# First two images of a channel-attention kernel in an order of their own, and one store an image

## The reference

```python
v = _gn(x)                                 # group norm: 32 groups of 12 channels
w = xt @ qkv_w.T                           # 384 x 384, for each of 1024 pixels
norm = sqrt(sum(w*w over pixels))          # for each channel
s = sum((w / norm)**2 over a head's 32 channels)
Pi = softmax(s * temp, over the 12 heads)  # for each pixel
Pi_n = Pi / (sum(Pi over pixels) + 1e-8)
dots = sum(Pi_n * w*w over pixels)         # for each channel
out = -(w * Pi) / (1 + dots)
y = x + out @ out_w.T + out_b
```

## Time and profile before

| | |
|---|---|
| median of three runs | 877.63 us |
| the profiled execution | 877.32 us |
| its span, first to last instruction | 875.4 us |
| PE busy | 855.1 us (98%) |
| DVE busy | 746.8 us (85%) |
| ACT, POOL busy | 528.0 us (60%), 225.5 us (26%) |
| DMA | 158.47 MB, mean 181 GB/s |

### The profile page before, as it was taken

How to read it: one execution, slowest core, us unless ns; L and a number is a source line. 1 busy time by engine, 2 the same in 40 slices (tenths; PEclk the granted TensorE clock), 3 DMA queues, 4 the chain that set the end, 5 groups by cost and what they waited for, 6 DMA issues and landing times.

```text
span 875.4 us, 14196 instructions
## 1 busy us (share of the span) xinstructions
PE 855.1 (98%) x4298; PEld 682.2 (78%) x4298; DVE 746.8 (85%) x1377; ACT 528.0 (60%) x676; POOL 225.5 (26%) x101
## 2 busy tenths in 40 slices
PE   6799999999999999999999999999999999999996
PEld 6577787777787777787777787777787777787785
DVE  7598888898888898888889888898888889888767
ACT  3575556676555676555676555677555677555631
POOL 1321233321233331233331133331133331133300
PEclk9899999999999999999999999999999999999999
DMA  7316655446655445665445665545664545664424
GB/s 279 113 42 220 225 167 192 149 178 215 224 185 192 144 176 201 224 198 179 155 170 196 224 204 173 164 171 187 224 218 159 176 160 187 222 224 153 132 74 165
DMA packets 54996, 158.47 MB, mean 181 GB/s; under 512 B 21442, under 2 KB 25794, under 8 KB 51010
## 3 DMA queue, kind: packets, MB, share of 16 engines
q1 hardware_dynamic: 46192, 155.48, 51.9%
q10 hardware_dynamic: 8786, 2.77, 1.3%
HBM read 105.70 MB, written 52.53 MB: 181 GB/s over the span
## 4 chain that ended last, share of the span: by engine, by line
PE 93%; DVE 3%; DMA 2%; issue 1%; ACT 1%; SPq 0%; DVEq 0%; ACTq 0%
PE acc L498 87%; PE scores L579 5%; DMA PIB<-pi 1%; DMA bias<-in_L_conv_out_b 1%; DVE WS L769 1%; DVE stats L656 0%; PE acc L481 0%; DVE XL L714 0%; DVE UL L841 0%; DMA pi<-PIT 0%; DVE WV L812 0%; DVE W2L L630 0%; DVE W1L L630 0%; ACT WV L408 0%; DVE XN L706 0%
## 5 line engine op out<-in xcount | busy, mean ns | idle before, releaser
L349 POOL TENSOR_TENSOR XL<-XN,XH 128x1024 fp32r<-128x1024 f32 x93 | 222.5, 2409 | 589.8 <-ACT XH L427 589.8
L399 ACT ACTIVATE WS<-acc 128x1024 f32<-128x1024 f32 x96 | 97.9, 1020 | 227.4 <-PE acc L498 213.2
L498 PE MATMUL acc<-XH,W1H 128*128 128x512 f32 x576 | 179.1, 392 | 3.9 <-ACT XH L427 3.7
L498 PE MATMUL acc<-UH,W2H 128*128 128x512 f32 x576 | 178.1, 390 | 2.6 <-ACT UH L389 2.5
L498 PE MATMUL acc<-XH,W1L 128*128 128x512 f32 x576 | 178.4, 391 | 0.0
L498 PE MATMUL acc<-UH,W2L 128*128 128x512 f32 x576 | 177.8, 390 | 0.0
L849 DVE SCALAR_TENSOR_TENSOR X<-acc,bias,X 128x1024 f32<-128x1024 f32 x95 | 118.8, 1276 | 38.0 <-PE acc L498 38.0
L498 PE MATMUL acc<-UL,W2H 128*128 128x512 f32 x576 | 149.9, 396 | 0.0
L769 DVE CUSTOM_DVE_ANT_0 WS<-PIB,WS 128x1024 f32<-128x1024 f32 x96 | 117.3, 1223 | 36.5 <-DMA PIB<-pi 35.8
L498 PE MATMUL acc<-XL,W1H 128*128 128x512 f32 x576 | 147.2, 391 | 0.2 <-DVE XL L714 0.2
L389 ACT ACTIVATE UH<-WV 128x1024 fp32r<-128x1024 f32 x96 | 98.1, 1054 | 78.3 <-DVE WV L795 61.2
(11 more groups left out here) (84 smaller groups left out, 439.9 us busy)
## 6 DMA issues: line engine op xcount, KB each, us to landing
PIB<-pi SPq DMA_DIRECT2D x96, 528.0 KB, 6.1
out_y<-X SPq DMA_DIRECT2D x95, 512.0 KB, 7.4
X<-in_x SPq DMA_DIRECT2D x31, 1536.0 KB, 6.3
gathered<-stats_rows ACTq DMA_DIRECT2D x30, 72.0 KB, 6.7
pi<-PIT SPq DMA_DIRECT2D x96, 16.5 KB
X<-in_x SPq DMA_DIRECT2D x3, 512.0 KB, 4.6
WV<-in_L_conv_qkv_w SPq DMA_DIRECT2D x1, 576.0 KB, 6.7
WS<-in_L_conv_out_w SPq DMA_DIRECT2D x1, 576.0 KB, 7.6
```

The lines of the kernel that those rows point to most:

```text
L349: pool.tensor_tensor(XL[:, t, :], XN[:, t, :], XH[:, t, :].bitcast(F32), ALU.subtract).then_inc(xl_done, 1)
L399: act.activation(square_tile(i, t), acc[:, t, :], ACT.Square, accum_out=sumsq[:, t:t + 1]).then_inc(squared, 1)
L498: last = pe.matmul(out[:, h * BANK:(h + 1) * BANK], w[:, k, m * P:(m + 1) * P], r[:, k, h * BANK:(h + 1) * BANK], start=(n == 0 and k == 0 ...
```

## The change

Outside the steps of images 0 and 1, only the stores differ: an image is stored by one DMA of 1.5 MB when its third tile is finished, instead of three of 512 KB; the last image keeps its stores by parts. Images 0 and 1 leave the common `step`, and each engine has a list of its own for them:

- PE starts the first product of image 0 ahead of the transposes of the second weight matrix, which now follow the six XH terms of tile 0. Images 0 and 1 do their XH terms early and their XL terms late (`opening_product`). The head sums of image 0 stand after the second k of tile 0 of image 1, those of image 1 after six `idle_turns`, ahead of all of image 0's second product, which goes in the order of k (`product_by_k`).
- The group means of images 1 and 2 come from small matmuls too; the first image whose statistics go through DRAM is image 3 (`BY_MATMUL`).
- DVE makes XN and XH of image 1, which ACT made. ACT makes a second copy of the turned second weights in SBUF (`minus_w2`), from which POOL makes W2L; DVE made it from PSUM. POOL makes one of the three XL tiles of image 0.
- Image 0 is weighed by tiles like the last image (`attend_tile`).

```diff
+MM_AGGREGATED, MM_MEANS, MM_OFFSET, MM_SPREAD, MM_VARIANCES = range(1, 6)
+BY_MATMUL = 3
...
-IDLE_TURNS = (6, 3, 1, 15)
+IDLE_TURNS = (6, 4, 6, 15)
...
+        def by_tiles(j):
+
+            return not j.follows(1) or has(j) and not has(j + 1)
...
-                store(i - 2, 2)
+                if not i.follows(2):
+                    spread_pi(i)
+                    return
+                store(i - 2)
                 if has(i - 2) and has(i + 2):
-                    sp.wait_ge(y_stored, (i - 2).counts(T * 16, T * 16))
+                    sp.wait_ge(y_stored, (i - 2).counts(16, 16))
                     load(i + 2)
                 spread_pi(i)
-                store(i - 1, 0)
-                store(i - 1, 1)
-
-            write_stats(sp, FIRST + 1)
-            gather_stats(sp, FIRST + 1)
-            pipeline(sp, step, 0, B)
+
+            step(FIRST)
+            step(FIRST + 1)
+            write_stats(sp, FIRST + BY_MATMUL)
+            gather_stats(sp, FIRST + BY_MATMUL)
+            pipeline(sp, step, 2, B)
...
+            pool.wait_ge(xn_done, T)
+            pool.wait_ge(xh_done, T)
+            pool.wait_ge(xl_done, T - 1)
+            pool.tensor_tensor(XL[:, T - 1, :], XN[:, T - 1, :], XH[:, T - 1, :].bitcast(F32),
+                               ALU.subtract).then_inc(xl_done, 1)
+            for k in range(T):
+                pool.wait_ge(w2_copied, k + 1)
+                pool.tensor_tensor(W2L[:, k, :], minus_w2[:, k, :], W2H[:, k, :].bitcast(F32),
+                                   ALU.subtract).then_inc(w2_lo, 1)
+            pool.wait_ge(xn_done, 2 * T)
+            step(FIRST)
+            step(FIRST + 1)
+            pipeline(pool, step, 2, B)
...
+            def w2_higher():
+
+                for k in range(T):
+                    act.wait_ge(weights_turned, T + k + 1)
+                    act.activation(W2H[:, k, :], turned(T + k), ACT.Copy, scale=-1.0).then_inc(weights_hi, 1)
+                    act.activation(minus_w2[:, k, :], turned(T + k), ACT.Copy, scale=-1.0).then_inc(w2_copied, 1)
...
+                    act.wait_ge(m1_done, i.counts(T, t + 1))
+                    if not i.follows(2) and i.follows(1):
+                        act.wait_ge(w2_lo, T)
...
+            def first_steps():
+
+                zero, one, two = FIRST, FIRST + 1, FIRST + 2
+                square_w(zero, 0)
+                keep_w(zero, 0)
+                group_seeds(one)
+                square_w(zero, 1)
+                square_w(zero, 2)
+                keep_w(zero, 1)
+                keep_w(zero, 2)
+                exponentials(zero)
+                square_w(one, 0)
+                keep_w(one, 0)
+                group_seeds(two)
+                square_w(one, 1)
+                square_w(one, 2)
+                keep_w(one, 1)
+                u_hi(zero, 0)
+                keep_w(one, 2)
+                u_hi(zero, 1)
+                u_hi(zero, 2)
+                exponentials(one)
+                for t in range(T):
+                    normalise(two, t)
+                    x_hi(two, t)
+
+            w1_higher()
+            for t in range(T):
+                x_hi(FIRST, t)
+            w2_higher()
+            first_steps()
+            pipeline(act, step, 2, B)
...
+            def opening_product(i, order, between):
+
+                for t, ns in order:
+                    if ns == (0, 1) and i.follows(1):
+                        pe.wait_ge(squared, i.counts(T, t + 1 - T))
+                        pe.wait_ge(w_kept, i.counts(T, t + 1 - T))
+                    for k in range(T):
+                        for n in ns:
+                            if t == 0 and n == 0:
+                                pe.wait_ge(xh_done, i.counts(T, k + 1))
+                            if t == 0 and n == 2:
+                                pe.wait_ge(xl_done, i.counts(T, k + 1))
+                            last = term(acc[:, t, :], t, (W1H, W1L), (XH, XL), n, k)
+                        if t == T - 1 and ns == (0, 1):
+                            last.then_inc(xh_read, 1)
+                        elif ns == (2,) and k == T - 1:
+                            last.then_inc(m1_done, 1)
+                        for other in between.get((t, ns, k), ()):
+                            other()
+
...
+            group_variances(FIRST)
             turn_weights(range(1, T))
             idle_turns(acc[:, T - 1, 0:P], IDLE_TURNS[1])
-            pe.wait_ge(w2_mixed, 1)
-            pe.wait_ge(temp_kept, 1)
-            pe.wait_ge(gn_step, GN_AGGREGATED)
-            turn_weights(range(T, 2 * T))
-            idle_turns(acc[:, T - 1, 0:P], IDLE_TURNS[2])
+
+            def turn_w2():
+
+                pe.wait_ge(w2_mixed, 1)
+                pe.wait_ge(temp_kept, 1)
+                pe.wait_ge(gn_step, GN_AGGREGATED)
+                turn_weights(range(T, 2 * T))
+
+            hi, lo = (0, 1), (2,)
             pe.wait_ge(weights_lo, T)
-            pipeline(pe, step, 0, B)
+            opening_product(FIRST, [(0, hi), (1, hi), (0, lo), (2, hi), (1, lo), (2, lo)],
+                            {(0, hi, 2): [turn_w2],
+                             (0, lo, 2): [lambda: pe.wait_ge(w2_copied, T)],
+                             (2, hi, 0): [lambda: group_means(FIRST + 1)],
+                             (2, hi, 2): [lambda: group_variances(FIRST + 1)]})
+            opening_product(FIRST + 1, [(0, hi), (1, hi), (2, hi), (0, lo), (1, lo), (2, lo)],
+                            {(0, hi, 1): [lambda: head_sums(FIRST)],
+                             (0, lo, 2): [lambda: group_means(FIRST + 2)],
+                             (1, lo, 2): [lambda: group_variances(FIRST + 2)]})
+            pe.wait_ge(gn_step, (FIRST + 2).counts(GN_STEPS, GN_AGGREGATED))
+            idle_turns(small[:, P:2 * P], IDLE_TURNS[2])
+            head_sums(FIRST + 1)
+            pe.wait_ge(w2_lo, T)
+            product_by_k(FIRST)
+            pipeline(pe, step, 2, B)
...
+            for t in range(T):
+                normalise(FIRST, t)
+            for t in range(T - 1):
+                x_lo(FIRST, t)
+            one, two, three = FIRST + 1, FIRST + 2, FIRST + BY_MATMUL
+            group_stats(one, range(T))
+            part_moments(one)
             dve.wait_ge(temp_kept, 2)
             dve.tensor_tensor(head_temp[:], head_mask[:], temp_o[:].unsqueeze(2).to_broadcast([P, T, QUAD]),
                               ALU.mult).then_inc(temp_kept, 1)
-            pipeline(dve, step, 0, B)
+            part_spreads(one)
+            moments_kept(one)
+            group_norm(one)
+            for t in range(T):
+                x_hi(one, t)
+            normalise(one, 0)
+            normalise(one, 1)
+            head_sum_weights(FIRST)
+            normalise(one, 2)
+            softmax_shift(FIRST)
+            softmax_divide(FIRST)
+            group_stats(two, range(T))
+            part_moments(two)
+            part_spreads(two)
+            moments_kept(two)
+            group_norm(two)
+            attend_tile(FIRST, 0)
+            head_sum_weights(one)
+            attend_tile(FIRST, 1)
+            attend_tile(FIRST, 2)
+            dve.memset(wait_cell[:], 0.0).then_inc(u_step, U_STEPS - T)
+            softmax_shift(one)
+            u_lo(FIRST, 0)
+            softmax_divide(one)
+            u_lo(FIRST, 1)
+            u_lo(FIRST, 2)
+            finish(FIRST, 0)
+            finish(FIRST, 1)
+            group_stats(three, range(T))
+            pipeline(dve, step, 2, B)
```

More of the change, by code:

```diff
@@ L220, in has, with tile_steps, scale_of, wait_weighed @@
             return not isinstance(j.number, int) or 0 <= j.number < B
[L222 to L226, removed]
+        def by_tiles(j):
+            return not j.follows(1) or has(j) and not has(j + 1)
+        def tile_steps(j, t, steps):
+            return (T * TILE_STEPS if j.follows(1) else 0) + TILE_STEPS * t + steps
+        def scale_of(t):
+            return dots[:, 3, t:t + 1]
+        def wait_weighed(eng, j, t):
+            if by_tiles(j):
+                eng.wait_ge(tile_step, tile_steps(j, t, TILE_STEPS))
+            else:
+                eng.wait_ge(u_step, j.counts(U_STEPS, ATTENDED + t + 1))
+        def in_blocks(tile):
+            return tile.rearrange("p (b n) -> p b n", n=QUAD)
         def norm_of(j):
@@ new lines, in x_hi @@
+            def x_hi(j, t):
+                if has(j):
+                    rstd_j, shift_j = norm_of(j)
+                    act.wait_ge(gn_step, j.counts(GN_STEPS, GN_STEPS))
+                    if j.follows(1):
+                        act.wait_ge(m1_done, j.counts(T))
+                        act.wait_ge(xl_done, j.counts(T, t + 1 - T))
+                    act.activation(XH[:, t, :], x_tile(j, t), ACT.Identity, bias=shift_j,
+                                   scale=rstd_j).then_inc(xh_done, 1)
@@ L442, in step, with exponentials @@
+            def exponentials(i):
+                if has(i):
```

(22 more changed lines are left out.)

281 lines of the change are left out of this document (126 added, 155 removed).

## The result

The changed kernel takes **878.58 us** (median of 20 runs, 878.11 to 880.31). The kernel before, in the same session, took 877.36 (20 runs, 876.57 to 877.85). The ratio is 1.0017 by the statistic used here throughout, 95% interval 1.0010 to 1.0024 (the two medians alone give 1.0014): 1.2 us lost, no gain. By the measure that the prediction set (0.2% is what can be told from no change) this sits inside the band of no change; with 20 runs a side the interval shows that it is a small loss. The forecast was 876.2. The profiled run took 879.03, its span 877.2.

What follows compares the result with a forecast made beforehand. PE bounds the kernel (93% of the chain), with gains only in the opening: head sums of image 2 at 80.6 against 81.83, 1.25 us gained. 877.32 - 1.25 = 876.07, or 876.38 by the median; taken 876.2, own range 875.2 to 877.3.

Steps and rivals of the forecast that it cites:

- XH on DVE: Opening, image 1: 0.75 us a tile, priced like XN with float32 output (806 ns), not the two-operand 1220 ns.
- rival 3: Opening: XH on DVE takes 1.22 us, delaying the head sums of image 0 by 1.4, to 877.6; chance 0.08.
- Head sums of image 0: Opening: DVE ends their weights at 32.0, PE stands 1.7 us and begins them at 32.1.
- The distance between the head sums of images 2 and 31: Steady steps: 29 x 26.16 = 758.6 us; the prediction is wrong if it is not met within 0.5.
- rival 2: Steady steps win too, as stores no longer run beside pi: 28 x 0.03 = 0.8 us, 875.4; chance 0.15.
- rival 4: Steady steps: single store ends too late, load misses statistics; beyond some 4 us late, each microsecond costs 28; chance 0.03.
- cost the single store at nothing: Steady steps: the later store moves the same bytes; the next load has 7.4 us of cover, less the landing.
- The low parts come at 57.3, 59.9 and 61.05: Second product of image 0: DVE's three UL, with image 1's softmax (2.5 us) between; product ends at 64.3, against 66.67.
- the paragraph on stores, POOL, ACT and SP: Other engines and queues: single store costs nothing, POOL's W2L ends near 24.3, long before 50; program's end unchanged.
- The prediction's own signs of being wrong: Clock at 0.50 from 30 to 67 us, head sums of image 2 after 81.9, or image 2-to-31 distance off 758.6.
- Rival 1: Clock falls in PE's 2.9 us gap before image 1's head sums: 877.9, or 879.9 if slow 11 us; chance 0.25.
- Rival 5: Opening: nothing won, since DVE sets the head sums of image 2 and small waits reach 1.2 us: 877.4; chance 0.07.

Runs made afterwards that it cites:

- the first experiment: Changed kernel, with POOL starting XL of image 2 only after DVE's last UL of image 0: 876.55 us, ratio 0.9994 to the kernel before.
- the second experiment: Changed kernel, with POOL starting XL of image 2 after DVE's second UL of image 0, the third yet to run: 876.58 us, ratio 0.9994.

## Why the prediction was wrong

**What held.** The first matmul of the products came at 14.42 (forecast 14.65). XH on DVE took 0.75 us a tile, at the price of XN, not of UL, so rival 3 falls. Head sums of image 0 at 32.28 (32.1), of image 1 at 49.04 (48.8); all stations within 0.3 us over 50 us of opening. The distance between the head sums of images 2 and 31 was 758.45 (758.6 within 0.5), so rival 2 falls, and rival 4 with it: the single store does not come late. That this number came out right is in part luck. The prediction took it that both kernels give PE the same steps and cost the single store at nothing; with three stores the changed order takes 761.1 to 761.7 us for them. The new order made the steady steps dearer, the single store made that good, and neither was in the sum. PE's waits for XH and the slow clock from 36 to 44 us are gone too: that mechanism was right.

**The step that failed** is "The low parts come at 57.3, 59.9 and 61.05", and the paragraph on stores, POOL, ACT and SP behind it, which of POOL weighs only W2L ("ends near 24.3, long before 50") and so puts its XL of image 2 at nothing without a reason. The first two came at 57.4 and 59.9. The third ended at 63.2, since POOL's XL of image 2 starts as soon as ACT has made its XH, 58.9 us, and nothing in the sum asked what POOL does then. In the kernel before, the same three XL ran from 59.96 to 67.5 us, and DVE had softmax, statistics and `finish` there, none of which they lengthened. The change moved DVE's low parts beside them. The size fits: 2.2 us on one instruction, in a stretch in which, as the prediction itself said, DVE sets the head sums of image 2. The forecast for these plus 2.2 is 82.8 (measured 83.37), and the first experiment, which takes only this away, gives 81.00 and 876.55 us, where 80.6 and 876.2 had been forecast. The rest of the sum up to these head sums was right to 0.4 us. The prediction's own signs of being wrong came true with it: these head sums after 81.9, and 0.50 on the clock.

The Trainium skill states the mechanism, and the prediction missed it: "SBUF — State Buffer", section "SBUF: two separate sides", says that DVE and GpSimd share a port pair under a lock held for the whole instruction, and that a DVE instruction with two SBUF inputs contends for it with a GpSimd instruction that reads SBUF. These runs agree: 3.42 us instead of 1.21, and the turn of roles in the second experiment. With the lengths measured here, a rival would have read: POOL's XL beside UL, up to one XL of 2.4 us late, an estimate of 876.2 + 2.4 = 878.6. That it meets the measured time so closely is chance: the hold was 2.2 us, and other terms were off by 0.4.

**Rival 1 happened and was not the cause.** The clock fell to 0.50 behind the gap of 2.77 us (2.9 forecast) and was back between 53 and 54. It had been priced at 1.7 us for 7 slow us. It lasted some 4 and cost 0.2 us at most where POOL was out of the way, because DVE was what the next stations waited for: PE's lateness disappeared in its wait for the low parts. That the forecast time of this rival, 877.9, lies near the result is chance; holding the clock alone made the kernel slower still. Rival 5 named the engine: DVE did set the head sums of image 2, but through one hold of 2.2 us and not through small waits.

## What to carry to other kernels

When instructions of DVE move, list what **POOL** executes at their new time, not only who signals whom: a DVE instruction with two inputs in SBUF, or a TENSOR_SCALAR between SBUF tiles, may stand behind a whole POOL instruction. It shows as a longer duration with no idle time before it, so compare the longest of a group with its mean; one wait that starts POOL later can cost nothing and give back all of it, as here. Before holding up a clock with idle work, ask whether the lateness is hidden at that place, and where PE will stand next. When two changes come together, take each out alone: here the store that bought nothing in the old order paid for the new one.

## What the runs showed of the hardware

- Some DVE instructions stand until a POOL instruction (here XL, a TENSOR_TENSOR that reads and writes SBUF) has ended, however small they are: 2.31 us for a TENSOR_SCALAR on 128x3 (0.16 in the changed kernel), 2.14 for a TENSOR_TENSOR on 128x96 (0.26 elsewhere), both with their inputs in SBUF. Others kept their durations beside POOL: RECIPROCAL (0.18), the statistics (0.68), `finish` (1.28) and a TENSOR_TENSOR of the softmax (0.27), the last two with an input in PSUM.
- PE's granted clock after a gap can go either way. After 2.27 empty us at the end of the kernel before it read 1.00 from 857 to 862; after 2.28 at the same place in the changed kernel it read 0.50 (below). After 2.77 us at 49 it fell, but after 2.76 at 54.97 in the kernel with the early XL of image 1 it stayed at 1.00, and one of the 20 executions of the changed kernel has a mean of 1.000, so the same program does both.

```profile
859.00:860.00 1.00, 1.00 (x3) 0.81 (x4) 0.64 (x4) 0.00 (x0) 0.00 (x0) 0.50 0.06 25
```

- A DVE TENSOR_SCALAR with fp32r output between SBUF tiles runs at 0.75 us for 1024 elements, as with a float32 output. The output type made no difference; UL, a TENSOR_TENSOR with a second operand of the same size, takes 1.22.
- One store of 1.5 MB in place of three of 512 KB took the wait for a small gather from 29.9 us to 0.2 over 29 steps of the old order, and the time of that kernel stayed where it was.
